# Attention on the two halves of TensorE's rows: two heads' products alternate, and a unit's query stack takes six transfers

## The reference

```python
xn = layernorm(x)
q = (xn @ wq).reshape(B, T, 32, 16);  k = xn @ wk;  v = xn @ wv          # k, v: B x T x 16
scores = einsum('bqhd,bkd->bhqk', q, k) * 0.25      # causal mask, softmax over keys
s = einsum('bhqk,bkd->bqhd', softmax(scores), v).reshape(B, T, 512) @ wo
h = linear8bit(xn, W1, b1); g = silu(linear8bit(h, W2, b2))               # 512 -> 2048 -> 512
out = x + s * g
```

## Time and profile before

| | us |
|---|---|
| median of 3 runs | 800.0 (799.98 to 802.72) |
| the profiled execution: its time | 802.84 |
| the profiled execution: span | 801.1 |
| PE busy, DVE busy, ACT busy, POOL busy | 764.9, 638.7, 402.7, 257.6 |
| granted TensorE clock, mean share of full speed | 0.979 |

### The profile page before, as it was taken

One profiled execution on the slowest core, in us unless ns is written; L12 is line 12 of the kernel. 1 busy time (PEld: TensorE's weight loads), 2 busy tenths in 40 slices (PEclk: granted clock), 3 DMA queues, 4 the chain that ended last, 5 costly groups with the idle time before them and its releaser, 6 DMA issues. The chain is left out here.

```text
span 801.1 us, 12089 instructions
## 1 busy us (share of the span) xinstructions
PE 764.9 (95%) x4253; PEld 579.5 (72%) x4253; DVE 638.7 (80%) x1094; ACT 402.7 (50%) x683; POOL 257.6 (32%) x335
## 2 busy tenths in 40 slices
PE   4999999999999999999999999999997999999995
PEld 3877665556676666775578888788886788888884
DVE  7988989999999899995537476666658998599957
ACT  3454166767677676777634554544553333122212
POOL 7313135555555555554621110110100000036504
PEclk9999589999999999999999999999999999999998
DMA  7421303333322223334554444222013778536982
GB/s 258 153 106 53 86 11 91 82 80 92 90 81 83 82 81 95 89 113 123 161 192 159 143 158 144 81 78 79 27 47 97 251 220 259 164 106 219 334 287 105
DMA packets 58348, 103.37 MB, mean 129 GB/s; under 512 B 8480, under 2 KB 16688, under 8 KB 56752
## 3 DMA queue, kind: packets, MB, share of 16 engines
q1 hardware_dynamic: 58288, 102.60, 40.3%
HBM read 52.76 MB, written 36.70 MB: 112 GB/s over the span
## 5 line engine op out<-in xcount | busy, mean ns | idle before, releaser
L914 DVE TENSOR_REDUCE rowmax<-ps 128x2 f32<-128x512 f32 (+3 forms) x384 | 210.9, 591 | 20.7 <-PE ps L991 18.8
L835 ACT ACTIVATE probs<-ps 128x512 f32<-128x512 f32 (+1 forms) x352 | 175.2, 557 | 72.4 <-PE ps L1004 70.7
L991 PE MATMUL ps<-km,stack 128*128 128x256 f32 (+3 forms) x512 | 151.0, 350 | 2.0 <-PEq L187 1.9
L1004 PE MATMUL ps<-stack,ks 128*128 128x512 f32 (+1 forms) x352 | 133.1, 388 | 2.6 <-ACT probs L835 2.6
L991 PEld LDWEIGHTS ps<-km,stack 128*128 128x128 f32 (+1 forms) x512 | 96.0, 201 | 42.2 <-DVE rowmax L914 22.5
L817 POOL TENSOR_SCALAR_AFFINE_SELECT probs<-probs 128x512 f32<-128x512 f32 x128 | 81.0, 641 | 79.1 <-ACT probs L835 77.6
L1806 PE MATMUL ps<-big_h 128*128 128x512 f32 x256 | 100.4, 392 | 2.4 <-issue 2.0
L1808 PE MATMUL ps<-big_h,big_l 128*128 128x512 f32 x256 | 100.3, 392 | 0.0
L1807 PE MATMUL ps<-big_l,big_h 128*128 128x512 f32 x256 | 100.2, 391 | 0.0
L1017 PE MATMUL ps<-probs,vones 128*32 128x512 f32 (+3 forms) x1024 | 82.2, 439 | 0.2 <-POOL probs L817 0.2
L1004 PEld LDWEIGHTS ps<-stack,ks 128*128 128x128 f32 x352 | 67.5, 192 | 11.9 <-ACT probs L835 6.3
(11 more groups left out here) (227 smaller groups left out, 1384.3 us busy)
## 6 DMA issues: line engine op xcount, KB each, us to landing
stack<-big_h SPq DMA_DIRECT2D x128, 64.0 KB, 2.0
h_scratch<-hs SPq DMA_DIRECT2D x7, 1024.0 KB, 4.5
hload<-h_scratch SPq DMA_DIRECT2D x14, 512.0 KB, 5.4
xn_scratch<-xa SPq DMA_DIRECT2D x4, 1024.0 KB, 4.4
stack<-big_l SPq DMA_DIRECT2D x64, 64.0 KB, 2.0
xi<-xn_scratch SPq DMA_DIRECT2D x16, 256.0 KB, 2.8
xe_scratch<-xm SPq DMA_DIRECT2D x16, 256.0 KB, 2.3
w2n<-in_L_ffn_W_dram SPq DMA_DIRECT2D x4, 1024.0 KB, 6.7
```

The lines of the kernel that those rows point to most:

```text
L835: nc.scalar.activation(probs[p][:, o:o + nh * w], ps[:, STB[n % NST], 0:nh * w], ACT.Exp).then_inc(s_exp, 1)
L914: nc.vector.tensor_reduce(dst, src, AX_X, ALU.max).then_inc(s_red, 1)
L991: last = nc.tensor.matmul(dst, stack[u % 3][rows, hp, P * qt:P * (qt + 1)], km[rows, u // KT, p0:p0 + npar, keys], start=True, stop=True)
L1004: ins = nc.tensor.matmul(ps[:, STB[n % NST], 0:nh * w].rearrange("p (h q) -> p h q", h=nh), ks[:, u // KT, p, P * kt:P * (kt + 1)], stack[ ...
```

## The change

The two heads of a pair leave the shared rows. Head `a` of each pair has its own half of the rows, 64a to 64a + 63: 48 rows of query parts, two of maxima, 14 of markers. `km` and `ks` exist once instead of twice. Every product covers one half of the rows, and products on the lower and the upper half alternate, into two different banks. To get this layout in 6 transfers of 16 rows x 4 pairs x 512, the columns of wq are stored by head, dimension, pair (`by_head`), and wo's rows are loaded in the matching order in 8 transfers.

A unit has 20 banks of maxima and 20 of scores (`CH, NB = 20, 10`), all 512 wide; steps come in pairs: at even steps TensorE issues a pair of banks and waits for both to be free. All tables of steps are set anew; PV's groups are key blocks (0, 1, 3) and (2,) instead of (0, 1) and (2, 3).

```diff
-        km = sa("km", [P, B, 2, T], F32R)
-        ks = sa("ks", [P, B, 2, T], F32R)
+        km = sa("km", [P, B, T], F32R)
+        ks = sa("ks", [P, B, T], F32R)
...
-            for hp in range(NPAIR):
-                src = slice(2 * HD * hp, 2 * HD * (hp + 1))
+            for a in range(2):
+                src = slice(HALF_ROWS * a, HALF_ROWS * (a + 1))
                 for n, part in enumerate((big_h, big_l, big_h)):
-                    sp.dma_start(stack[u % 3][2 * HD * n:2 * HD * (n + 1), hp, :].bitcast(F32),
-                                 part[src, f, tok].bitcast(F32)).then_inc(s_sq[u % 3][hp], 16)
+                    lo = HALF_ROWS * a + HD * n
+                    sp.dma_start(stack[u % 3][lo:lo + HD, :, :].bitcast(F32),
+                                 part[src, f, tok].bitcast(F32)).then_inc(s_sq[u % 3], 16)
...
-                        for p in range(2):
-                            step(nc.vector.tensor_scalar(km[:, g, p, :], kvh, cols[:, p:p + 1], None,
-                                                         ALU.mult))
+                        step(nc.vector.tensor_scalar(ks[:, g, :], kvh, cols[:, 0:1], None, ALU.mult))
...
-        CH = 24
+        CH, NB = 20, 10
+        def pieces_of(c):
+            v, m = divmod(c // 2, 5)
+            hp = 2 * v + m // 2
+            if m == 4:
+                return [(2 * v + h, 1, own, 2 * P * h + P * own) for h in range(2) for own in (False, True)]
+            if m % 2:
+                return [(hp, 2, False, 0), (hp, 2, True, 2 * P), (hp, 0, True, 3 * P)]
+            return [(hp, 3, False, 0), (hp, 3, True, 3 * P)]
+        def scores_of(i):
+            return [[(0, 0, 1, 0)], [(0, 1, 1, 0)], [(1, 0, 1, 0), (3, 0, 1, 3 * P)],
+                    [(1, 1, 1, 0), (3, 1, 1, 3 * P)], [(2, 0, 2, 0)]][i]
+        GROUPS = [(0, 1, 3), (2,)]
...
-        LAG = 11
+        LAG = 10
-        PV_AT = {11: (0, 0), 16: (0, 1), 22: (1, 0), 27: (1, 1)}
+        PV_AT = {10: (0, 0), 14: (0, 1), 18: (1, 0), 22: (1, 1)}
...
+                def max_pair(u, c):
+                    if n + 1 >= NMAX:
+                        pe.wait_ge(s_red, n + 2 - NMAX)
+                    pieces = pieces_of(c)
+                    for hp, qt, own, at in pieces:
                         keys = slice(P * qt, P * qt + P) if own else slice(0, P * qt)
+                        for a in range(2):
+                            rows = slice(HALF_ROWS * a, HALF_ROWS * a + (HALF_ROWS if own else KEPT))
+                            dst = ps[:, MAXB[(n + a) % NMAX], at:at + keys.stop - keys.start]
+                            ins = nc.tensor.matmul(dst, stack[u % 3][rows, hp, P * qt:P * (qt + 1)],
+                                                   km[rows, u // KT, keys], start=True, stop=True)
+                def score_pair(u, s):
+                    if n + 1 >= NST:
+                        pe.wait_ge(s_exp, n + 2 - NST)
+                    for kt, h, nh, at in parts:
+                        for a in range(2):
+                            rows = slice(HALF_ROWS * a, HALF_ROWS * (a + 1))
+                            ins = nc.tensor.matmul(dst, ks[rows, u // KT, P * kt:P * (kt + 1)],
+                                                   stack[u % 3][rows, 2 * p + h:2 * p + h + nh, P * kt:T],
```

More of the change, by code:

```diff
@@ L149, in block_layernorm_attention_ffn @@
         s_ks = sem("score_keys_ready")
-        s_sq = [[sem(f"stack{i}_queries{hp}") for hp in range(NPAIR)] for i in range(3)]
+        s_sq = [sem(f"stack{i}_queries") for i in range(3)]
         def stack_queries(sp, u):
@@ L271, in steps_along @@
                                                  base=-SPARE, pattern=[[0, P]], channel_multiplier=1))
+                    step(nc.gpsimd.tensor_copy(tile[HALF_ROWS + 2 * HD:P, :], tile[2 * HD:HALF_ROWS, :]))
                 steps_along(later_q, [STEP ** -s for s in range(RUN)] + [0.0])
-                steps_along(later_k, [-STEP ** t for t in range(RUN + 1)])
                 fill_spare(0).then_inc(s_z, 1)
                 pool.wait_ge(s_z, 1)
+                steps_along(later_k, [-OWN * STEP ** t for t in range(RUN + 1)])
                 for g in range(B):
@@ L525, in block_layernorm_attention_ffn @@
         NP_ = NPAIR * sum(T - P * k for k in range(QT))
+        OF_1, OF_2 = NPAIR * T, 2 * NPAIR * T
         probs = [sa(f"probs{p}", [P, NP_]) for p in range(2)]
-        P_OFF = [NPAIR * sum(T - P * j for j in range(k)) for k in range(QT)]
-        rowmax = sa("rowmax", [P, 2, QT + 2, HPF])
-        row_hl = sa("row_hl", [P, 2, QT, 2, HPF])
+        rowmax = sa("rowmax", [P, 2, QT + 3, HPF])
+        row_hl = sa("row_hl", [P, 2, QT, 2, 2, NPAIR])
         ta = sa("ta", [P, T // 32, 32])
@@ L976, in max_piece @@
                         pe.wait_ge(s_z, u + 1)
-                    if m == 0:
-                        pe.wait_ge(s_sq[u % 3][hp], 16 * 3 * (u // 3 + 1))
-                    if n >= NMAX:
-                        pe.wait_ge(s_red, n - NMAX + 1)
-                    bank, o = ps[:, MAXB[n % NMAX], :], 0
-                    for qt, own, p0, npar in PIECES[m]:
-                        rows = slice(0, P if own else 6 * HD)
-                        keys = slice(P * qt, P * qt + P) if own else slice(0, P * qt)
-                        w = keys.stop - keys.start
-                        if m == 1:
-                            dst = bank.rearrange("p (a k) -> p a k", a=2)[:, :, keys]
-                        else:
-                            dst = bank[:, o:o + npar * w].rearrange("p (a k) -> p a k", a=npar)
-                        o += npar * w
-                        last = nc.tensor.matmul(dst, stack[u % 3][rows, hp, P * qt:P * (qt + 1)],
-                                                km[rows, u // KT, p0:p0 + npar, keys], start=True, stop=True)
@@ L993, in max_piece @@
-                    last.then_inc(s_max, 1)
-                def scores(u, s):
-                    p, i = divmod(s, NB)
-                    kt, h0, nh = BANKS[i]
-                    w = T - P * kt
+                    if c == 0:
+                        pe.wait_ge(s_sq[u % 3], 16 * 6 * (u // 3 + 1))
+                    if n + 1 >= NMAX:
+                        pe.wait_ge(s_red, n + 2 - NMAX)
+                    pieces = pieces_of(c)
+                    for hp, qt, own, at in pieces:
+                        keys = slice(P * qt, P * qt + P) if own else slice(0, P * qt)
+                        for a in range(2):
+                            rows = slice(HALF_ROWS * a, HALF_ROWS * a + (HALF_ROWS if own else KEPT))
+                            dst = ps[:, MAXB[(n + a) % NMAX], at:at + keys.stop - keys.start]
+                            ins = nc.tensor.matmul(dst, stack[u % 3][rows, hp, P * qt:P * (qt + 1)],
+                                                   km[rows, u // KT, keys], start=True, stop=True)
+                            if (hp, qt, own, at) == pieces[-1]:
+                                ins.then_inc(s_max, 1)
@@ L1057, in _ @@
                 for g in range(STEPS):
-                    if g < CH * U:
-                        max_piece(*divmod(g, CH))
+                    if g < CH * U and g % 2 == 0:
+                        max_pair(*divmod(g, CH))
                     u, s_ = scored(g)
-                    if 0 <= u < U and s_ < 2 * NB:
-                        scores(u, s_)
+                    if u >= 0 and s_ % 2 == 0:
+                        score_pair(u, s_)
                     for at, (p, group) in PV_AT.items():
```

207 lines of the change are left out of this document (105 added, 102 removed).

## The result

The changed kernel takes **854.8 us** (median of 4 runs, 854.16 to 856.92) against 801.0 for the kernel before beside it: a ratio of **1.067** (95% interval 1.0655 to 1.0688), 54 us slower. The forecast was 788 us, with a range of 770 to 824. It was wrong in sign and in size. The profiled execution took 854.36 us, span 852.2, mean granted clock 0.934 against 0.979.

The account below looks back on a forecast made before the run. PE was taken to bound a unit (18.3 us), VectorE right behind. Units -11.5, start -0.8 and preparation +0.3 sum to -12.0: 802.84 gives 790.8 profiled, 788 us as the runs' median; range 770 to 824.

Parts of the forecast that it names:

- the one on transfers: Query transfers on SP: six of twice the size, issued seven us ahead, stay hidden even if landing doubles to 4 us.
- The clock: Rival: half-row products leave the attention stage's clock low, PE needing about 26 us a unit; 3 in 100.
- Concurrent couples: Max and score products: lower-half and upper-half products run together, 5.9 us a unit instead of 9.3, minus 3.4; chance 0.52.
- loads in line: Rival: the array takes one weight load at a time, worst in max_pair; 20.0 us a unit, 824 us; chance 0.14.
- no concurrency: Rival: max and score couples run serially, 11.7 us instead of 9.3, 860 us; chance 0.09 including low clock.
- Turns: Projection and maxima's transposes between half-row products: 0.35 us per change of array shape and back, plus 1.75 us a unit.
- The unit: Attention unit period: PE and DVE 16.6 us each, 0.9 us of DVE starving; 17.5 us against 18.3.
- coupling eats it: Rival: every PV group starves DVE for its full 0.9 us; unit 18.3 us, no change, 800 us; chance 0.11.
- no turn cost: Rival: array turns in attention are free, PE at 14.9 us, DVE alone bounds at 16.6; 776 us; chance 0.14.
- The number of units: Maxima stage: 263 us at 18.3 make 14.4 units, each 0.8 us shorter, minus 11.5 us.
- The start: First 35 max steps, at DVE's pace, become 30 of 0.6 us: minus 0.8 us.
- Preparation: Before the first maxima: scaling saved on DVE buys nothing, two more short copies; taken +0.3 us, between -2 and +2.

Follow-up runs that it names:

- e4: The kernel before, with a unit's first max product waiting for all twelve query transfers instead of its pair's three; 824.8 us, ratio 1.0303.
- e3: The changed kernel with eleven unused 512-column products before the wait for the stack, from unit 3 on; 844.1 us, ratio 1.0535.
- e6: e2 with six rotating banks instead of three for the first 24 max banks; 809.0 us, ratio 1.0108.
- e15: e12 with three more unused full-row products at each of steps 20, 22, 24 and 26; 799.4 us, ratio 0.9995.
- e9: e6 with three extra full-row products at four steps of units 1 to 7; 824.3 us, ratio 1.0291.
- e12: e6 with a pair's halves waiting apart and unused products behind the step's own, until projection begins; 804.7 us, ratio 1.0054.
- e5: e2 with each max product of units 1 to 7 issued twice; 836.9 us, ratio 1.0470.
- e8: e2 with all max products of a pair's lower half issued first, then all of the upper half; 814.1 us, ratio 1.0179.
- e2: The changed kernel with the six query transfers issued two steps earlier, ahead of the load of `xi` on SP; 812.4 us, ratio 1.0152.
- e13: e12 with the pair's single wait kept; 805.2 us, ratio 1.0058.
- e14: The kernel before with one extra product behind each of its first 24 max pieces; 800.0 us, ratio 0.9991.

## Why the prediction was wrong

**The step that failed** is the one on transfers: "issued at step 51 for use at 60 (seven us ahead); doubled to 4 us they stay hidden". I counted one transfer's landing and doubled it for its size. What counts is the run of six: 3.2 us until the last is issued and 5.5 until it lands, 8.7 us, against 6.2 from the first issue (257.41) to the end of PE's last work before the pair (263.56). The 2.5 us between are the stall. The kernel before would have failed the same count (9.0 against 7.9 us), had its first product needed the whole stack, as e4 shows (+24 us). That the new layout makes it need all six transfers, where three of twelve had been enough, had no price in my forecast, nor had the time that the issues take one after another. By the Trainium skill (DMA: Bandwidth & Descriptors, Anatomy of one DMA) a transfer issued by GpSimd costs about 2.0 us plus its bytes at 436 GB/s, which makes an estimate of 2.3 us for 128 KB. SyncE's transfers of 64 KB, before, are near that formula (2.0), the 128 KB in a run of six aren't (4.8 in the median, 5.5 for the last), while the DMA engines are 93% busy.

**The clock.** I gave 3 in 100 to a low clock and saw it as a trait of half-row products. It came in another way: through stalls, and through the thin work of early units, which with faster products leaves PE idle. The 1.2 us or more a unit that e3 shows, and the 10 us between e6 and e15, had no term in my sum. The early units lose their clock where the faster products, the gain that I forecast, leave PE idle beside DVE, and the added work of e9, e12 and e15 holds it. Why that of e5 didn't stays open.

**Concurrent couples: right.** Two products of a couple start 2 to 4 ns apart in the record of after (254 to 267 us), mostly 10 to 13 in e8. Four couples of 128 columns go in 0.50 us (262.62 to 263.12), 0.12 each against my 0.11. The rivals of loads in line (824) and no concurrency (860) are out as mechanisms, though after's time lies nearest to the latter.

**Turns: right.** The score couple ahead of a projection triple holds PE 0.38 us (256.71 to 257.09), the triple's first product 0.34 and its last 0.33 (257.66 to 257.99), each 0.23 by its columns: 0.15 + 0.11 + 0.10, or 0.36 against my 0.35.

**The unit: right, 17.4 in e2 and 17.3 in e15 against 17.5**, and by the terms of the sum. The steady stretch of e2, and DVE's wait for max products from 280 to 350 us, four units:

```profile
300.00:350.00 50.00, 48.22 (x477) 27.48 (x475) 47.19 (x92) 36.19 (x69) 28.83 (x39) 1.00 0.48 90
```

```profile
DVE rowmax L942 <- PE ps L1015: 3.1, 8, 0.4
```

Per unit that is PE 16.8 us (I had 16.6), DVE 16.5 (16.6), and DVE starved for 0.8 in two waits of 0.4 (I had taken 0.9 out of 0 to 1.8). Of the rivals on it, "coupling eats it" (18.3) and "no turn cost" (16.6) are out.

**The number of units: mis-sized.** I took 18.3 for all of 263 us. Only the units with projection take that; units 2 to 5 take 17.5 to 17.6 and win 0.2 at most, not 0.8, and unit 1 loses even in e15 (17.5 against 15.8). e15's whole maxima stage is 272.4 us against 281.8: 9.4 less, where I had 12.3.

**The start: mis-sized.** The first units were to win 0.8; with pairs over three banks unit 0 loses 3.2 (16.2 against 13.0), and e6 turns that into the 0.8 (12.2). I had used this very coupling for PV's steps and not for the start.

**Preparation** +3.6, outside my bounds of 2. **After the last maxima** +1.6 and +0.7, within them.

Put together, e15 is my forecast with the transfers, the banks and the clock mended: -9.4 in maxima, +3.2 in preparation, +1.5 to the last PV and +0.7 to the feed-forward, +0.2 in it, -3.8 of span. So with the failed step, the banks and the clock mended, the change comes to 799 us on the profiled execution (802.84 less 3.8), not 788. The ratio of e15, 0.9995 with 1 in its interval, says that this is no difference that can be measured.

## What to carry to other kernels

Price a group of transfers from its first issue to the landing of its last, and take that landing from a run of such transfers, not from one alone; compare it with the time to the *first* use. When a new layout makes the first product need all of the transfers instead of a few, redo that count even if the bytes stay. TensorE made faster beside an engine that bounds idles more, and here its clock took the gain back in the early units: look in each stage at what else keeps TensorE fed. Work put between a wait and the product that releases another engine cost most of its time (units 3 to 5 take 19.7 us in e9, for twelve products of 0.23 us); the same work behind the step's own products cost nothing here (17.4 in e13).

## What the hardware showed beyond that

- Larger transfers in a run gained little: 768 KB arrived 8.7 us after the first issue in six pieces, 9.0 us in twelve, with the DMA engines 93% and 51% busy.
- Unused products can pay: e15 issues 132 more than e6 does (4,865 against the 4,733 of after), and stands 9.7 us under it, of which e13 and e12 put 0.5 down to the split waits.
- Removing low clock isn't worth time by itself. e14 has 20 us less of it than the kernel before, and gains 1.5 us at most by its interval: unit 1 is faster (15.8 to 14.0), unit 0, where DVE bounds, isn't (13.0 to 13.6).
- Half-row products of one side, several in a row in the kernel's order, run beside those of the other side that come behind them: in e8 eight of 128 columns give way to the next product after 0.51 us (300.52 to 301.03), as in the alternating order of e2 (0.50).
